# Graph convolution with an LSTM cell on one core: a third dense group, and another layout and order for the span one-hots

## The chip, the cores and the metric

One core of one Trainium2 chip runs the kernel. The metric is the device time of one execution in microseconds (us). The kernel before takes 1732.85 us, the median of 3 runs (1732.84 to 1735.09).

## The reference, cut to what matters

N = 6250 nodes with 256 features, 200,000 edges sorted by destination. The destinations are drawn as `6250 * u ** 2`, so low nodes have most edges: of 25 groups of 250 nodes, group 0 has about 40,000, group 1 16,600, group 2 12,700, group 3 10,700 and group 24 4,000.

```python
agg = segment_sum(x[src], dst, num_segments=N)
h = relu(agg @ W_rel + b_rel + x @ W_root)            # 512 wide
i, f, g, o = split(h @ W_ih.T + b_ih + b_hh, 4)
c = sigmoid(i) * tanh(g)
y = (sigmoid(o) * tanh(c)) @ W_fc + b_fc              # 256 wide
out = layernorm(x + y)
```

## The kernel before, in words

Edges lie in chunks of 128, one edge a partition. A **step** is 4 chunks (QC = 4). A **turn** handles one group of 250 nodes (two tiles of 125); 25 turns run one after the other, and in turn n each engine also does the second half (gates, last layer, layer norm) of the group of turn n - 1.

The sum over a node's edges is made in two ways.

**Tile groups** (23 of 25). GpSimd (POOL) gathers for each step four blocks of 128 rows of x, each split into a high and a low part (four indirect DMAs, L352), into a ring of RING = 7 steps. VectorE (DVE) builds a one-hot of each step against the 125 nodes of the tile (`visit`, L825), and TensorE (PE) multiplies the one-hots with the rows (L424, four matmuls of 512 columns a visit). A tile is done in two parts, so a turn has four parts, in **gaps** j = 0 to 3; a step on a tile's border is visited twice. SyncE forwards the landings (L309). POOL issues step s once PE has begun step s - 7.

**Dense groups** (DENSE = 2: groups 0 and 1). For these PE builds a count matrix `adj` (sources by 250 nodes). A **span** is 5 nodes, a **window** two spans (10 nodes, 25 windows a group), a **pair** one step of a span: DVE makes `rel` (L812), `hot_lo` (128 x 4 chunks, L814) and `hot_key` (245 x 4 chunks, L817), all 16 bit, into a ring of PAIRS = 4. PE multiplies them, four matmuls of 245 columns a pair (L399), into a PSUM bank; a window starts with a clearing matmul (L386) and ends with a marker (L379), and ScalarE (ACT) copies the bank to `adj` (L588). In both tiles the four chunks are innermost, so one chunk's columns lie 8 bytes apart. When the group's 25 windows are done, `product_batch` (L412) multiplies `adj` with x, loaded in 7 batches (896 KB each, `load_batch`) into the space of `hot_key`: batches 0 to 3 in one turn, 4 to 6 in the next, and then comes the dense group's own turn. Each batch is 28 recorded matmuls.

**Order in a gap j of turn n.** PE: `part_sum(j)`, `gates(n-1, j)` (L485, 24 recorded matmuls), the windows of this gap, a batch if there is one. After gap 3: hidden layer (L467, L472), last layer (L493), transposes (L455). DVE: `part_hots(j)`, in gap 0 `normalise(n-2)` (L877 to L888), then `add_high`, `cell_product(n-1, j-1)`, `out_gate(n-1, j-2)` (L846 to L855), and last the windows of the gap (`windows_at`); after gap 3 `norm_stats(n-1)` (L859 to L873), whose sum L864 marks the end of a turn. ACT has the matching order; `store(n-2)` comes after its gap 1. `part_hots` waits until PE has used every one-hot of the part before. Three windows (31 pairs) are built before turn 0.

`SLOTS = (2, 1, 1, 1)` says how many windows each gap of a window turn takes. Counted from the indices, turn by turn (T = tile steps newly consumed, P = pairs in the four gaps, B = batches; 282 steps, 327 visits and 163 pairs in all, POOL issuing 287 steps, a multiple of 7):

```
turn  0: T 25 P 11,4,4,4    turn  7: T 6 (dense 0)        turn 14: T 10 B 3
turn  1: T 21 P 8,4,4,4     turn  8: T 6  P 4,2,2,2       turn 15: T 5 (dense 1)
turn  2: T 19 P 8,4,4,4     turn  9: T 12 P 4,2,2,2       turn 16: T 4
turn  3: T 17 P 6,3,3,3     turn 10: T 12 P 4,2,2,2       turn 17: T 10
turn  4: T 15 P 0,0,2,2     turn 11: T 12 P 4,2,2,2       turns 18-20: T 9 each
turn  5: T 14 B 4           turn 12: T 11 P 4,2,2,2       turns 21-24: T 8 each
turn  6: T 14 B 3           turn 13: T 10 B 4
```

A turn with four parts has T + 2 visits, a turn with two parts T + 1. In group 0 a span has 1 to 9 pairs, in group 1 one pair for nearly all spans.

## Time and profile before

| | |
|---|---|
| median of 3 runs | 1732.85 us |
| the profiled execution | 1737.03 us, span 1735.2 us |
| PE busy / POOL busy / DVE busy / ACT busy | 83% / 73% / 41% / 21% |
| mean granted TensorE clock | 0.915 |

The rows further down come from the page of the profile, from its view by stretches (busy time of each engine between two times), and from its instructions in order of time. PE is TensorE's matmuls, PEld its weight loads. In a row of the timeline, "[1.35 <-DVE hot_key L817]" is the idle time of that engine before the row and what ended it; "x8" is how many instructions the row merges.

Borders of stretches were put at starts of L864, the end of a turn: turn 6 ends at 787.0, turn 8 at 876.7, turn 11 at 1066.8, turn 12 at 1129.7, turn 14 at 1265.3, turn 15 at 1302.1, turn 16 at 1337.9, turn 20 at 1526.3, turn 24 at 1695.9.

### The profile page before, as it was taken

To read this page: it belongs to the slowest core of one execution; us is meant where nothing else is said; L and a number is where in the kernel's file an instruction comes from. 1 tells how busy PE (TensorE), PEld (TensorE's weight loads), DVE (VectorE), ACT (ScalarE), POOL (GpSimd) and SP (SyncE) were. 2 spreads that over 40 slices of the span, in tenths; PEclk is the share of its full clock that TensorE was granted. 3 is DMA by queue.
4 is the path that set the end of the run, shared out by engine and by line. 5 is a ranking of instruction groups with operands and counts; after the bars stand their busy time and mean duration, and the time that the engine had idled before them with its cause. 6 is when DMAs were issued, how large, how long until landed. Compare 5 with 4: busy or idle time off the path is not lost.

```text
span 1735.2 us, 28751 instructions
## 1 busy us (share of the span) xinstructions
PE 1435.9 (83%) x6194; PEld 1128.6 (65%) x6195; DVE 708.4 (41%) x1482; ACT 372.3 (21%) x697; POOL 1263.1 (73%) x1464
## 2 busy tenths in 40 slices
PE   0266557687787789899989889989999999999997
PEld 0133345364555568788777667678888877788886
DVE  8966325255262332213554554422233333333332
ACT  0000011021121221213323223222133222223333
POOL 3668778788787877777757787665763778778772
PEclk9996568798887899899989989999999999999999
DMA  8776676776677778887747667666764677777773
GB/s 272 276 240 183 197 203 192 200 207 187 198 207 199 215 208 270 244 254 218 201 145 216 201 198 216 175 212 213 246 193 120 201 220 213 217 216 214 214 219 90
DMA packets 135705, 360.45 MB, mean 208 GB/s; under 512 B 20207, under 2 KB 58636, under 8 KB 134006
## 3 DMA queue, kind: packets, MB, share of 16 engines
q0 software_dynamic: 91840, 301.01, 59.4%
q10 hardware_dynamic: 39864, 41.96, 7.7%
q1 hardware_dynamic: 3936, 16.62, 2.5%
q8 instruction: 40, 0.66, 0.1%
q14 instruction: 25, 0.20, 0.0%
HBM read 340.31 MB, written 19.20 MB: 207 GB/s over the span
## 4 chain that ended last, share of the span: by engine, by line
PE 34%; POOL 22%; DMA 19%; issue 13%; DVE 6%; DVEq 4%; ACT 1%; POOLq 1%; SPq 0%; ACTq 0%
POOL rows L352 21%; DMA rows<-x_parts,idx 17%; PE ps_blk L485 11%; PE ps_agg L424 6%; PE ps_win L412 4%; PE ps_y L493 3%; PE ps_blk L467 3%; PE ps_blk L472 3%; PE ps_win L399 2%; DMA hot_key<-in_xb 2%; DVEq L812 1%; POOL idx L338 1%; DVE hot_key L817 1%; DVEq L802 1%; DVE rows L694 1%
## 5 line engine op out<-in xcount | busy, mean ns | idle before, releaser
L352 POOL DMA_INDIRECT rows<-x_parts,idx x1148 | 1154.3, 1005 | 398.1 <-issue 320.9
L485 PE MATMUL ps_blk<-cell,wih_sb 128*128 128x250 f32 x2400 | 544.8, 384 | 2.2 <-issue 1.6
L424 PE MATMUL ps_agg<-rows,onehot 128*125 x1308 | 396.8, 454 | 144.6 <-SPq L309 127.0
L485 PEld LDWEIGHTS ps_blk<-cell,wih_sb 128*128 128x128 f32 x2400 | 461.8, 195 | 71.4 <-issue 12.8
L424 PEld LDWEIGHTS ps_agg<-rows,onehot 128*125 128x125 f32 x1308 | 265.3, 209 | 238.4 <-issue 183.9
L825 DVE SCALAR_TENSOR_TENSOR onehot<-iota_f,tile_first,dst_u 128x500 f32 x327 | 242.1, 742 | 328.2 <-PE ps_agg L424 224.5
L613 ACT ACTIVATE cell<-ps_blk,bg_sb 128x250 f32<-128x250 f32 x300 | 140.5, 469 | 526.6 <-PE ps_blk L485 526.6
L399 PE MATMUL ps_win<-hot_key,hot_lo 128*128 x516 | 127.9, 397 | 67.4 <-DVE hot_key L817 60.7
L399 PEld LDWEIGHTS ps_win<-hot_key,hot_lo 128*128 x516 | 59.0, 115 | 126.1 <-issue 90.6
L812 DVE TENSOR_SCALAR rel<-key,span_key x163 | 42.2, 259 | 163.7 <-issue 128.4
L817 DVE TENSOR_TENSOR hot_key<-iota_h,rel 128x980 f16 x163 | 108.0, 663 | 0.1
L467 PE MATMUL ps_blk<-x_t,wroot_sb 128*128 128x250 f32 x400 | 99.1, 380 | 0.1
L472 PE MATMUL ps_blk<-cell,wrel_sb 128*128 128x250 f32 x400 | 94.8, 379 | 0.0
L412 PE MATMUL ps_win<-adj,hot_key 128*128 128x250 f32 x392 | 88.5, 384 | 6.9 <-DMA hot_key<-in_xb 6.9
L493 PE MATMUL ps_y<-wfc_sb,cell 128*125 128x256 f32 x400 | 90.4, 379 | 0.0
L846 DVE TENSOR_TENSOR agg_n<-ps_agg,agg_n 125x256 f32<-125x256 f32 x46 | 19.3, 420 | 170.9 <-ACT agg_n L593 170.9
L412 PEld LDWEIGHTS ps_win<-adj,hot_key 128*128 128x128 f32 x392 | 76.0, 195 | 17.9 <-DMA hot_key<-in_xb 8.8
L850 DVE TENSOR_TENSOR cell<-cell 128x250 f32<-128x250 f32 x100 | 41.9, 419 | 107.6 <-ACT cell L613 107.6
L593 ACT ACTIVATE agg_n<-ps_agg 125x256 f32<-125x256 f32 x46 | 17.6, 383 | 312.8 <-PE ps_agg L379 312.8
L472 PEld LDWEIGHTS ps_blk<-cell,wrel_sb 128*128 128x128 f32 x400 | 73.9, 189 | 12.8 <-ACT cell L597 5.0
L493 PEld LDWEIGHTS ps_y<-wfc_sb,cell 128*125 128x125 f32 x400 | 75.0, 187 | 11.1
L467 PEld LDWEIGHTS ps_blk<-x_t,wroot_sb 128*128 128x128 f32 x400 | 74.3, 192 | 8.9 <-issue 1.0
(113 smaller groups left out, 744.5 us busy)
## 6 DMA issues: line engine op xcount, KB each, us to landing
rows<-x_parts,idx POOLq DMA_INDIRECT x1148, 3.7
hot_key<-in_xb ACTq DMA_DIRECT2D x14, 896.0 KB, 7.2
x_t<-in_xT ACTq DMA_DIRECT2D x25, 250.0 KB, 3.7
x_n<-in_x ACTq DMA_DIRECT2D x25, 250.0 KB
out<-y ACTq DMA_DIRECT2D x25, 250.0 KB
x_parts<-rows SPq DMA_DIRECT2D x6, 1024.0 KB, 4.7
rows<-in_x ACTq DMA_DIRECT2D x8, 512.0 KB, 10.6
x_parts<-wih_sb SPq DMA_DIRECT2D x2, 1024.0 KB, 3.8
```

The lines of the kernel that those rows point to most:

```text
L352: g.indirect_dma_start(rows_f[:, k * QC + j, :], None, x_parts, bass.IndirectOffsetOnAxis(ap=idx[:, k, j:j + 1], axis=0)).then_inc(landed[ ...
L399: last = mm(o, hot_lo[:, ds(half, 1), :, j].squeeze(1), hot_key[:, ds(half, 1), :, j].squeeze(1), start=False, stop=False)
L412: last = mm(ps_win[:, c * GN:(c + 1) * GN], xs[:, b, c * P:(c + 1) * P], adj[:, i * X_BATCH + b, :], start=(i == 0 and b == 0 and c == 0), ...
L424: ins = mm(o, onehot[:, hot * QC + j, 0:TN], rows[:, ds(slot + j, 1), :].squeeze(1), start=(first and j == 0), stop=False)
L467: mm(ps_blk[m % BANKS][:, 0:GN], wroot_sb[:, k, m * P:(m + 1) * P], x_t[:, k, :], start=(k == 0), stop=False)
L472: last = mm(ps_blk[m % BANKS][:, 0:GN], wrel_sb[:, k, m * P:(m + 1) * P], agg_t[:, k, :], start=False, stop=(k == KI - 1))
L485: last = mm(o, wih_sb[:, k, col:col + P], h_t[:, k, :], start=(k == 0), stop=(k == KH - 1))
L493: last = mm(ps_y[0:TN, a * D_OUT:(a + 1) * D_OUT], sig_o[:, k, a * TN:(a + 1) * TN], wfc_sb[:, k, :], start=(k == 0 and a == 0), stop=(k = ...
L613: nc.scalar.activation(dst[:, j, :], ps_blk[b % BANKS][:, 0:GN], fn, bias=bg_sb[:, bias + j:bias + j + 1]).then_inc(gate_done, 1)
L812: v.tensor_scalar(rel[:, ds(half, 1), :].squeeze(1), key[:, ds(c, QC)], span_key[:, at:at + 1] if static else span_key[:, ds(at, 1)], None ...
L817: v.tensor_tensor(hot_key[:, ds(half, 1), :, :].squeeze(1), iota_h[:, :, :], rel[:, ds(half, 1), :].to_broadcast([P, SCOLS, QC]), ALU.is_e ...
L825: v.scalar_tensor_tensor(onehot[:, ds(hot, QC), 0:TN], iota_f[:, 0:TN].unsqueeze(1).to_broadcast([P, QC, TN]), nodes, dst_u[:, ds(c, QC)]. ...
```

## The change

1. DENSE = 3: group 2 is computed by count matrix and product too, its tile steps are gone. There are 25 more windows with 50 pairs, and 7 more batches. TILES falls from 46 to 44 and SPANS rises from 100 to 150, which the table built at the start follows.
2. Group 0's windows go two to each gap (`FIRST_SLOTS`), all others one to each gap.
3. `hot_lo`, `hot_key` and `iota_h` hold two chunks innermost and have an outer dimension of two (PQ) for the other two: a chunk's columns lie 4 bytes apart. The element count of each DVE instruction is as before.
4. DVE builds the windows of a gap directly behind `part_hots`, ahead of `normalise`, `add_high`, `cell_product` and `out_gate`. `normalise` moves to gap 1 and ACT's `store` behind its gap 2.

PE's order within a turn is unchanged. Counted again (258 steps, 301 visits, 213 pairs; POOL issues 259 steps):

```
turn 0: T 22 P 11,8,8,8    turn  7-9: T 12 P 2,2,2,2      turn 16: T 10 P 2,2,2,2
turn 1: T 19 P 8,8,8,7     turn 10: T 11 P 2,2,2,2        turn 17-19: T 9 P 2,2,2,2
turn 2: T 17 P 3,3,6,4     turn 11: T 11 P 2,2,2,4        turn 20: T 8 P 2,2,2,4
turn 3: T 15 B 4           turn 12: T 10 B 4              turn 21: T 8 B 4
turn 4: T 14 B 3           turn 13: T 10 B 3              turn 22: T 8 B 3
turn 5: T 7 (dense 0)      turn 14: T 5 (dense 1)         turn 23: T 4 (dense 2)
turn 6: T 7 P 2,2,2,2      turn 15: T 4 P 2,2,2,2         turn 24: T 4, two parts
```

```diff
-DENSE = 2
+DENSE = 3
-SLOTS = (2, 1, 1, 1)
+FIRST_SLOTS, SLOTS = (2, 2, 2, 2), (1, 1, 1, 1)
+PQ = QC // 2
-            wins = list(SLOTS)
+            wins = list(SLOTS if k > 0 else FIRST_SLOTS)
-        iota_h = sb("iota_h", [P, SCOLS, QC], f16)
+        iota_h = sb("iota_h", [P, SCOLS, 2], f16)
-        hot_lo = sb("hot_lo", [P, PAIRS, P, QC], f16)
-        hot_key = sb("hot_key", [P, PAIRS, SCOLS, QC], f16)
+        hot_lo = sb("hot_lo", [P, PAIRS, PQ, P, 2], f16)
+        hot_key = sb("hot_key", [P, PAIRS, PQ, SCOLS, 2], f16)
...
-                                last = mm(o, hot_lo[:, ds(half, 1), :, j].squeeze(1), hot_key[:, ds(half, 1), :, j].squeeze(1), start=False, stop=False)
+                                last = mm(o, hot_lo[:, ds(half, 1), j // 2, :, j % 2].squeeze(1), hot_key[:, ds(half, 1), j // 2, :, j % 2].squeeze(1), start=False, stop=False)
...
-                    if j == 1 and g2 is not None:
+                    if j == 2 and g2 is not None:
                         store(n - 2, g2)
...
-                    v.tensor_tensor(hot_lo[:, ds(half, 1), :, :].squeeze(1), iota_h[:, 0:P, :],
-                                    src_lo[:, ds(c, QC)].unsqueeze(1).to_broadcast([P, P, QC]), ALU.is_equal)
+                    v.tensor_tensor(hot_lo[:, ds(half, 1), :, :, :].squeeze(1), iota_h[:, 0:P, :].unsqueeze(1).to_broadcast([P, PQ, P, 2]),
+                                    src_lo[:, ds(c, QC)].rearrange("p (q c) -> p q c", c=2).unsqueeze(2).to_broadcast([P, PQ, P, 2]), ALU.is_equal)
                     dve.wait_ge(rel_made, s + 1)
-                    v.tensor_tensor(hot_key[:, ds(half, 1), :, :].squeeze(1), iota_h[:, :, :],
-                                    rel[:, ds(half, 1), :].to_broadcast([P, SCOLS, QC]), ALU.is_equal).then_inc(pairs_ready, 1)
+                    v.tensor_tensor(hot_key[:, ds(half, 1), :, :, :].squeeze(1), iota_h[:, :, :].unsqueeze(1).to_broadcast([P, PQ, SCOLS, 2]),
+                                    rel[:, ds(half, 1), :].squeeze(1).rearrange("p (q c) -> p q c", c=2).unsqueeze(2).to_broadcast([P, PQ, SCOLS, 2]),
+                                    ALU.is_equal).then_inc(pairs_ready, 1)
...
                     if parts[j] is not None:
                         part_hots(t, *parts[j])
-                    if j == 0 and back >= 2:
+                    windows_at(w, wins, j)
+                    if j == 1 and back >= 2:
                         normalise(n - 2)
...
                     if j == KH - 1 and parts[j] is not None and parts[j][1] == 1:
                         add_high(t, parts[j][0])
-                    windows_at(w, wins, j)
```

## Rows read from the trace of the kernel before

**Rows 1.** The page, busy us of each engine with share and instruction count.

```profile
PE 1435.9 (83%) x6194; PEld 1128.6 (65%) x6195; DVE 708.4 (41%) x1482; ACT 372.3 (21%) x697; POOL 1263.1 (73%) x1464
```

**Rows 2.** The page, costliest groups: busy us, mean ns of one | idle before.

```profile
L352 POOL DMA_INDIRECT rows<-x_parts,idx x1148 | 1154.3, 1005 | 398.1 <-issue 320.9
...
L825 DVE SCALAR_TENSOR_TENSOR onehot<-iota_f,tile_first,dst_u 128x500 f32 x327 | 242.1, 742 | 328.2 <-PE ps_agg L424 224.5
...
L399 PE MATMUL ps_win<-hot_key,hot_lo 128*128 x516 | 127.9, 397 | 67.4 <-DVE hot_key L817 60.7
...
L817 DVE TENSOR_TENSOR hot_key<-iota_h,rel 128x980 f16 x163 | 108.0, 663 | 0.1
```

**Rows 3.** View by stretches of POOL's L338 alone, one for each step issued.

```profile
80.60:767.10 686.50, 32.45 (x126) 0.83 0.72 213
226.70:767.10 540.40, 24.39 (x101) 0.86 0.73 214
```

**Rows 4.** View by stretches, all engines: borders, length, PE, PEld, DVE, ACT, POOL, clock, DMA.

```profile
876.70:1066.80 190.10, 173.91 (x768) 133.05 (x766) 91.85 (x204) 54.37 (x93) 143.76 (x168) 0.93 0.68 196
1129.70:1265.30 135.60, 130.12 (x594) 111.95 (x593) 33.81 (x73) 25.65 (x52) 87.08 (x106) 0.97 0.72 223
1265.30:1302.10 36.80, 36.80 (x175) 32.07 (x174) 12.10 (x29) 12.92 (x26) 23.50 (x29) 1.00 0.67 192
1526.30:1695.90 169.60, 165.36 (x762) 139.68 (x761) 62.35 (x136) 51.31 (x104) 134.98 (x161) 1.00 0.74 216
```

**Rows 5.** Timeline of PE in turn 15: start us, us, line, operation.

```profile
1270.70 3.08 PE L424 MATMUL ps_agg<-rows,onehot 128*125 x12
1273.62 10.31 PE L485 MATMUL ps_blk<-cell,wih_sb 128*128 128x250 f32 x48
```

**Rows 6.** Timeline of PE in turn 13, the first two product batches.

```profile
1148.59 9.12 PE L412 MATMUL ps_win<-adj,hot_key 128*128 128x250 f32 x28 [5.30 <-DMA hot_key<-in_xb]
...
1165.55 6.07 PE L412 MATMUL ps_win<-adj,hot_key 128*128 128x250 f32 x28
```

**Rows 7.** Timeline of PE in turn 11, windows of gap 0 and of gap 2.

```profile
1021.49 1.04 PE L399 MATMUL ps_tr<-hot_key,hot_lo 128*128 x4 [1.35 <-DVE hot_key L817]
1024.34 1.04 PE L399 MATMUL ps_tr<-hot_key,hot_lo 128*128 x4 [1.81 <-DVE hot_key L817]
...
1026.55 5.39 PE L424 MATMUL ps_agg<-rows,onehot 128*125 x12 [1.17 <-DVE onehot L825]
...
1047.93 1.92 PE L399 MATMUL ps_win<-hot_key,hot_lo 128*128 x8
```

**Rows 8.** Timeline of DVE in turn 11: normalise, two pairs, two one-hots.

```profile
1011.78 0.17 DVE L877 RECIPROCAL r<-std 125x2 f32<-125x2 f32 x1 [1.01 <-ACT std L622]
...
1014.84 0.23 DVE L812 TENSOR_SCALAR rel<-key,span_key  x1 [1.33 <-issue]
...
1017.41 0.23 DVE L812 TENSOR_SCALAR rel<-key,span_key  x1 [1.23 <-issue]
...
1047.02 0.74 DVE L825 SCALAR_TENSOR_TENSOR onehot<-iota_f,tile_first,dst_u 128x500 f32 x1 [0.42 <-issue]
1048.10 0.74 DVE L825 SCALAR_TENSOR_TENSOR onehot<-iota_f,tile_first,dst_u 128x500 f32 x1 [0.35 <-issue]
```

**Rows 9.** Timeline of DVE before turn 0, two pairs of one span.

```profile
101.26 0.23 DVE L812 TENSOR_SCALAR rel<-key,span_key  x1 [0.32 <-issue]
...
102.79 0.23 DVE L812 TENSOR_SCALAR rel<-key,span_key  x1 [0.32 <-issue]
```

**Rows 10.** One line, L386, 900 to 1130 us: min/median/max ns, first and last start.

```profile
L386 PE MATMUL ps_win<-zero_bf x15: 267/267/268, 910.3 to 1121.5; 128*128 128x245 bf16 x15
```

**Rows 11.** Timeline of DVE at the start, first of four instructions over 100 spans.

```profile
18.15 1.82 DVE L713 TENSOR_TENSOR adj<-chunk_stat,adj 98x1600 f32<-98x1600 f32 x1
```

**Rows 12.** Timeline of DVE, the last two ends of turns.

```profile
1695.94 0.69 DVE L864 TENSOR_TENSOR y<-ps_y,x_n 125x512 f32<-125x512 f32 x1 [3.10 <-PE ps_y L493]
...
1726.32 0.69 DVE L864 TENSOR_TENSOR y<-ps_y,x_n 125x512 f32<-125x512 f32 x1 [1.23 <-PE ps_y L493]
```

More of the change, by code:

```diff
@@ L157, in gnn_kernel @@
         rel = sb("rel", [P, PAIRS, QC], f16)
-        hot_lo = sb("hot_lo", [P, PAIRS, P, QC], f16)
-        hot_key = sb("hot_key", [P, PAIRS, SCOLS, QC], f16)
+        hot_lo = sb("hot_lo", [P, PAIRS, PQ, P, 2], f16)
+        hot_key = sb("hot_key", [P, PAIRS, PQ, SCOLS, 2], f16)
         adj = sb("adj", [P, SRC_HI, GN])
-        xs = hot_key[:, :, :, :].rearrange("p s k c -> p (s k c)")[:, 0:2 * X_BATCH * D_IN].bitcast(f32).rearrange("p (b d) -> p b d", b=X_BATCH)
+        xs = hot_key[:, :, :, :, :].rearrange("p s q k c -> p (s q k c)")[:, 0:2 * X_BATCH * D_IN].bitcast(f32).rearrange("p (b d) -> p b d", b=X_BATCH)
         agg_n = sb("agg_n", [TN, 2, D_IN])
@@ L320, in _ @@
             g.iota(iota_f[:, :], pattern=[[1, P]], base=0, channel_multiplier=0, **imprecise).then_inc(const_made, 1)
-            g.iota(iota_h[:, :, :], pattern=[[1, SCOLS], [0, QC]], base=0, channel_multiplier=0, **imprecise).then_inc(const_made, 1)
+            g.iota(iota_h[:, :, :], pattern=[[1, SCOLS], [0, 2]], base=0, channel_multiplier=0, **imprecise).then_inc(const_made, 1)
             g.memset(zero_bf[:, :], 0.0).then_inc(const_made, 1)
```

## The prediction

> **What bounds the kernel now.** I read the page first: PE is busy 83% of the span and POOL 73% [rows 1], so neither is plainly the bound. POOL's own share misleads: it is busy 1005 ns in each of 1148 gathers [rows 2], but there is a fixed issue time between them. The view by stretches, of the one instruction that POOL runs a step, tells more: 101 steps in 540.4 us, 5.35 us a step, from 227 to 767 us [rows 3]. That is the pace of a POOL that is never held up. The 25 turns then fall in two kinds. Where tile steps times 5.35 us is more than PE's own work, the turn takes POOL's time (turns 21 to 24: 32 steps, 171 us by this rule, 169.6 measured [rows 4]). Where it is less, the turn takes PE's time (turn 15: 5 steps would be 27 us, it takes 36.8 with PE busy throughout at full clock [rows 4]). The reader should see that a group made dense takes steps from POOL and gives work to PE and DVE; so what matters is where in the order each is the bound.
>
> **PE's prices at full clock.** Three visits take 2.92 us (12 matmuls from 1270.70 until L485 starts at 1273.62 [rows 5]), 0.98 each. Turn 15 has 6, so its rest is 36.8 - 5.9 = 30.9 us; with transposes, which a dense turn lacks, 31.5. A product batch is 6.0 us of PE, and the first of a group waited 5.3 for its load [rows 6]: a product is 7 x 6.0 + 5.3 = 47.3. Check: turns 13 and 14 give 2 x 31.5 + 24 x 0.98 + 47.3 = 133.8; measured 135.6 [rows 4].
>
> A window of two ready pairs has 8 matmuls in 1.92 us [rows 7], 0.22 each, with clear and marker about 2.2 us. The same 245 columns take 267 ns from start to end where they lie next to each other [rows 10] and 397 where they lie 8 bytes apart [rows 2]: 130 ns more, about what 245 columns need a second time at 2.4 GHz. So the 8 byte pitch streams at half rate. The change makes it 4 bytes, which no 16 bit row shows. The nearest is the tile matmul: 512 columns of 4 byte words in 0.98 / 4 = 0.245 us [rows 5], full rate. I take full rate, 0.11 a matmul, 1.4 us a window; the other end is no gain, 2.2.
>
> The Trainium skill (SBUF — State Buffer, "Door 1: The DMA port swizzle") says of lines of 16 bytes that two hits on each are enough for full bandwidth. By that the old layout, with two, is already at full rate, and the new one brings nothing; the 397 against 267 ns of the trace speak against it. By the rule the sum would be the second rival's.
>
> **DVE's prices.** Within a span a pair comes every 1.53 us [rows 9]; a span of one pair takes 2.56, since the loop is entered anew [rows 8]. So a window of groups 1 and 2 costs DVE 5.1 us, more than PE. A part of three visits costs 1.0 to enter and 1.1 each [rows 8], 4.3. A normalise is about 2.1 [rows 8], each cell or out operation 0.4. The element counts don't change. The new second input of L814 and L817 repeats one 4 byte word where it repeated 8 bytes. The nearest row: L825 repeats one 16 bit element for each of 125 columns and takes 742 ns for 500 elements [rows 2], about one element a cycle. So I take no extra cost; the other end is 0.5 us a pair (below).
>
> **Part by part.** (a) *Start.* Four instructions over 100 spans of 1.82 us [rows 11] get 150: their length is nearly all elements, so 0.9 us more each, some 3.7 in all. DVE works without a break until x is split, so gathers and pairs start 3.7 later. The smaller `iota_h` saves POOL time that nobody waits for.
>
> (b) *Turns 0 to 11, POOL's.* In 686.5 us POOL issued 125 steps besides the first [rows 3], its early stall at the full ring included. After the change 159 steps are consumed through turn 11. 80.6 + 3.7 + 686.5 + 34 x 5.35 = 952.7. From the last step's issue to the end of its turn there are 20 us (767.1 [rows 3] against the end of turn 6 at 787.0). That makes 973. Turns 0 and 1 now have 35 and 31 pairs: DVE needs 16 x 2.56 + 15 x 1.53 = 64 us for those of turn 1, 27 for its visits and some 11 for normalise, cell operations and layer norm, and only four pairs can be made ahead while PE is in its gates, so about 110 us against POOL's 19 x 5.35 = 102. The ring of 7 takes most of this; I add 5 (bounds 0 and 15): **turn 11 ends at 978**, against 1066.8 before. The other turns stay POOL's: turns 7 to 9 need 64 of POOL and 31.5 + 14 x 0.98 + 5.6 = 50.8 of PE, some 56 of DVE.
>
> (c) *Turns 12 to 24, no longer POOL's.* POOL needs 10 steps or less in each. Turns 12 and 13: 133.8. Turn 14: 30.9 + 6 x 0.98 = 36.8. Turn 15 (5 visits, 4 windows): 31.5 + 4.9 + 5.6, and 2 for DVE, 44. Turn 16 with 12 visits and 4 windows would be 48.9 by PE. But DVE's gap 1 is 4.3 + 5.1 + 2.1 + 0.4 = 11.9 and its gap 2 is 10.6, PE's 2.9 + 5.2 + 1.4 = 9.5. `part_hots` of the next gap is queued behind these, so PE finds no one-hot at gaps 2 and 3, by 1.7 and 1.3 us. That is 52. The same reckoning gives 60 for the turns before of 12 steps, which took 190.1 / 3 = 63.4 [rows 4], so I add 1: 53. Turns 17 to 19: 52 each; turn 20, with two windows in its last gap, 54. Turns 21 and 22: 2 x 31.5 + 20 x 0.98 + 47.3 = 129.9. Turns 23 and 24: 30.9 + 4.9 and 31.5 + 4.9 = 72.2. Sum: 133.8 + 36.8 + 44 + 53 + 156 + 54 + 129.9 + 72.2 = **679.7**, with 2 more for waits on steps as turn 12 begins. The same thirteen turns took 1695.9 - 1066.8 = 629.1 before. DVE's new order costs nothing else: `cell_product` and `normalise` come later, but ACT's tanh and the store are needed only at the turn's end. In gap 0 the build of pairs no longer waits behind `normalise`, and the 1.35 + 1.81 + 1.17 us of idle PE of the double window [rows 7] go.
>
> (d) *Tail.* 1695.94 to 1726.32 and then to the end at 1735.2 [rows 12]: 39.3, unchanged.
>
> Sum: 978 + 681.7 + 39.3 = 1699 us of span, 36 less than 1735.2. The profiled execution took 1737.0 with what lies around its span, the median of runs 1732.85. So the forecast in terms of the median is 1732.85 - 36 = 1697; rounded with the DVE waits being the softer side, **1698 us**. In short: about 89 us saved while POOL is the bound, 53 given back once PE and DVE are.
>
> **Rivals.**
> *One: DVE is not late in turns 15 to 20.* Then these take PE's time: 2 + 4 + 12 + 6 less, and the 5 of turns 0 and 1 go too: 29 less, **1669**. For: `part_hots` could overlap better than I think where slots are free. Against: the same reckoning came out too low before.
> *Two: the layout doesn't do what it says, a matmul stays at 0.22 us.* A window is 0.8 longer; of 25 windows in the PE stage DVE's lateness hides most, 5 to 20 us: **1703 to 1718**. For: no row shows 16 bit columns 4 bytes apart.
> *Three, slower: the repeated single word costs DVE 0.5 us a pair.* The 31 early pairs delay PE, and POOL behind the full ring, by 15.5. Turns 0 and 1, already DVE's, pass on some 20 of their 33. Turns 15 to 20 have 50 pairs, 21 to 25 us. Together 56 to 60: **1754 to 1758**. It decides from 0.3 us a pair on, where the gain of 35 is used up. Against: L825's 742 ns. If the two-at-a-time rate of L817 (980 elements in 663 ns [rows 2]) were lost altogether it would be 0.8 a pair and more, some 1785.
>
> The Trainium skill (Vector Engine (DVE) Microarchitecture Reference, "5.2 Measured stream behaviour on trn2") says that a port keeps its full rate only while elements come in runs of two or more neighbouring 4 byte words. The new repeated input is one such word. By its figures (1.05 against 1.73 ns a column) I estimate 0.5 us a pair: rival three. Whether a word read again counts as a hop no run here shows.
>
> **How the numbers follow.** Forecast 0.52 (own range 1685 to 1715), rival one 0.14, rival two 0.11, rival three 0.15, and 0.08 for a chain that I haven't seen at 1720 to 1740. Faster: 0.52 + 0.14 + 0.11 and half of the last, 0.81; within 0.2% (about 3.5 us, what a measurement of this kernel can tell) 0.03; slower 0.16. Range 1668 to 1745: it leaves out most of rival three and the low edge of rival one.
>
> **What would show it.** Right: L399's mean falls from 397 to some 280 ns; L817 stays near 663; L352 x1036; turn 11 ends near 978 and the thirteen turns after it take about 680; in turns 16 to 20 PE waits for L825 at gaps 2 and 3; POOL's pace is above 5.35 us a step after turn 11. Wrong: L814 or L817 longer, POOL with long stalls before turn 2, or waits for hot_key in the single windows.

## The result

The changed kernel takes 1717.6 us (median; 1711.7 to 1732.5), the kernel before beside it 1733.1. The ratio is 0.991, 95% interval 0.990 to 0.993: 15.5 us faster, where the forecast said 35. The profiled execution has a span of 1716.0 us against 1735.2, 19.2 less. The experiments fall in two sets. In the first (e1 to e6, e9, e10) the kernel before takes 1730 and 1733 us. In the second (e7, e12, e14 to e21) it takes 2242 to 2251 us, on three chips, one of which is the chip of e1 to e4. Between the sets only ratios to the kernel before and single rows are compared here, and an experiment's time is set beside the 1717.6 only in the first set. That comparison is across chips too, so each ratio stands with it.

The page of after (busy us, mean ns of one | idle before), to be read beside [rows 1] and [rows 2]; all line numbers are 1 to 2 higher than before:

```profile
PE 1431.2 (83%) x6531; PEld 1150.2 (67%) x6532; DVE 762.2 (44%) x1604; ACT 395.2 (23%) x720; POOL 1154.3 (67%) x1324
...
L353 POOL DMA_INDIRECT rows<-x_parts,idx x1036 | 1047.7, 1011 | 428.5 <-issue 370.7
...
L400 PE MATMUL ps_win<-hot_key,hot_lo 128*128 x656 | 106.8, 301 | 67.5 <-DVE hot_key L818 61.5
...
L818 DVE TENSOR_TENSOR hot_key<-iota_h,rel 128x980 f16 x213 | 141.2, 663 | 0.0
...
L413 PE MATMUL ps_win<-adj,hot_key 128*128 128x250 f32 x588 | 127.9, 375 | 1.9 <-DMA hot_key<-in_xb 1.6
L815 DVE TENSOR_TENSOR hot_lo<-iota_h,src_lo 128x512 f16 x213 | 113.7, 534 | 1.3 <-issue 1.3
```

POOL gave up 112 gathers and 109 us of busy time. The window matmul fell from 397 to 301 ns, `hot_key` stayed at 663, `hot_lo` rose from 483 to 534.

The view by stretches of after, borders at ends of turns (L866), columns as in [rows 4]. The rows are turns 9 to 11, 12 and 13, 14, 15, 17 to 19, and all of 12 to 24:

```profile
806.20:997.50 191.30, 160.98 (x742) 129.46 (x741) 87.78 (x191) 51.61 (x91) 153.15 (x176) 0.95 0.72 205
997.50:1126.10 128.60, 126.92 (x594) 110.20 (x593) 34.18 (x72) 25.65 (x52) 84.75 (x104) 1.00 0.75 231
1126.10:1163.00 36.90, 36.90 (x175) 32.13 (x174) 12.21 (x30) 12.93 (x26) 22.59 (x29) 1.00 0.67 192
1163.00:1213.50 50.50, 44.06 (x208) 36.33 (x207) 22.61 (x52) 15.96 (x28) 16.59 (x20) 0.93 0.36 100
1266.90:1423.80 156.90, 143.51 (x704) 116.95 (x703) 79.20 (x178) 50.62 (x90) 123.10 (x141) 1.00 0.71 202
997.50:1677.00 679.50, 645.57 (x3063) 545.11 (x3062) 256.06 (x578) 190.37 (x359) 399.28 (x471) 0.99 0.62 181
```

So turn 11 ended at 997.5 instead of the 978 forecast, and turns 12 to 24 took 679.5 against 681.7 forecast. By turns, forecast and measured: 12 and 13 133.8 + 2 and 128.6; 14 36.8 and 36.9; 15 44 and 50.6; 16 53 and 53.3; 17 to 19 156 and 156.9; 20 54 and 58.2; 21 and 22 129.9 and 123.2; 23 and 24 72.2 and 71.9. The tail is 39.0.

POOL's own pace in after, L339 alone, one start for each step issued, as in [rows 3]:

```profile
84.20:782.50 698.30, 33.84 (x126) 0.88 0.73 212
84.20:966.90 882.70, 43.29 (x160) 0.89 0.73 211
```

The forecast put the last of these 160 starts at 952.7; it is at 966.8. Three intervals stand out, 8.5, 7.3 and 9.7 us, behind the ends of turns 1, 3 and 6. The last of them, with PE's first tile matmuls of turn 7, then POOL's next gather:

```profile
687.09 4.05 PE L425 MATMUL ps_agg<-rows,onehot 128*125 x16
...
689.38 0.97 POOL L353 DMA_INDIRECT rows<-x_parts,idx  x1 [4.78 <-issue]
```

Counted from the indices, this gather is of step 108 (the first is 0), which may be issued once PE has begun step 101, the first of turn 7. In all three places the waiting gather starts 2.3 us after PE's first tile matmul of the new turn (360.61 and 362.89, 533.00 and 535.27, 687.09 and 689.38). So POOL stood at the full ring while PE was in the hidden and last layers around the end of a turn. The kernel before has no interval above 6.5 us between 227 and 767 us.

PE in after, turn 17 with the start of its window in gap 3; then the last two windows of turn 11, both in gap 3 (columns as in [rows 7]):

```profile
1280.76 0.27 PE L387 MATMUL ps_win<-zero_bf 128*128 128x245 bf16 x1
1280.86 1.05 PE L400 MATMUL ps_win<-hot_key,hot_lo 128*128 x8
1281.75 0.17 PE L380 MATMUL ps_win<-zero_bf 128*128 128x1 bf16 x1
1283.11 3.24 PE L425 MATMUL ps_agg<-rows,onehot 128*125 x12 [1.20 <-DVE onehot L827]
...
1304.81 2.20 PE L425 MATMUL ps_agg<-rows,onehot 128*125 x8 [1.19 <-issue]
...
1312.63 0.27 PE L387 MATMUL ps_win<-zero_bf 128*128 128x245 bf16 x1
...
1313.77 1.95 PE L468 MATMUL ps_blk<-x_t,wroot_sb 128*128 128x250 f32 x8
```

```profile
984.50 0.27 PE L387 MATMUL ps_win<-zero_bf 128*128 128x245 bf16 x1
...
987.05 0.74 PE L400 MATMUL ps_tr<-hot_key,hot_lo 128*128 x4 [1.27 <-issue]
989.28 0.74 PE L400 MATMUL ps_tr<-hot_key,hot_lo 128*128 x4 [1.48 <-issue]
...
990.37 3.53 PE L468 MATMUL ps_blk<-x_t,wroot_sb 128*128 128x250 f32 x8
```

Two things are to be seen. Eight matmuls of a single window now take 1.05 us instead of 1.92 [rows 7]. Yet the next part starts 2.35 us after the clear (1283.11 - 1280.76), and it was 2.34 before (medians: 8 single windows in turns 9 to 12 before, 15 in turns 16 to 20 after): what the matmuls saved stands as idle time behind the marker, 1.20 us. And a second window in the last gap is dear: 5.87 us from its first clear to the hidden layer, where a single window there takes 1.14, and the hidden layer then runs at half clock, 3.53 us for 8 matmuls instead of 1.95 (granted clock 0.55 from 990.3 to 994.0).

### The profile page after: what moved, and what is told of

Its sections match the earlier page's. It is cut to its first block, busy times and chain, and to the rows that moved or that the text cites. A ratio compares the mean times of both kernels' runs of the same rounds, so it can differ in the third digit from the quotient of the medians.

```text
span 1716.0 us, 30403 instructions
## 1 busy us (share of the span) xinstructions
PE 1431.2 (83%) x6531; PEld 1150.2 (67%) x6532; DVE 762.2 (44%) x1604; ACT 395.2 (23%) x720; POOL 1154.3 (67%) x1324
## 4 chain that ended last, share of the span: by engine, by line
PE 43%; POOL 18%; issue 15%; DMA 12%; DVE 6%; DVEq 5%; POOLq 1%; ACT 0%; SPq 0%; ACTq 0%
POOL rows L353 17%; PE ps_blk L486 17%; DMA rows<-x_parts,idx 11%; PE ps_agg L425 8%; PE ps_win L413 5%; PE ps_y L494 4%; PE ps_blk L468 4%; PE ps_blk L473 2%; PE ps_win L400 2%; DVEq L813 1%; POOL idx L339 1%; DMA hot_key<-in_xb 1%; DVE hot_key L818 1%; PE ps_tr L400 1%; DVE rows L695 1%
## 5 line engine op out<-in xcount | busy, mean ns | idle before, releaser
L353 POOL DMA_INDIRECT rows<-x_parts,idx x1036 | 1047.7, 1011 | 428.5 <-issue 370.7
L425 PE MATMUL ps_agg<-rows,onehot 128*125 x1204 | 344.3, 437 | 117.1 <-SPq L310 78.6
L425 PEld LDWEIGHTS ps_agg<-rows,onehot 128*125 128x125 f32 x1204 | 233.7, 200 | 193.0 <-issue 148.3
L827 DVE SCALAR_TENSOR_TENSOR onehot<-iota_f,tile_first,dst_u 128x500 f32 x301 | 223.1, 743 | 249.0 <-PE ps_agg L425 163.3
L400 PE MATMUL ps_win<-hot_key,hot_lo 128*128 x656 | 106.8, 301 | 67.5 <-DVE hot_key L818 61.5
L818 DVE TENSOR_TENSOR hot_key<-iota_h,rel 128x980 f16 x213 | 141.2, 663 | 0.0
L400 PEld LDWEIGHTS ps_win<-hot_key,hot_lo 128*128 x656 | 64.9, 99 | 105.6 <-issue 84.3
L413 PE MATMUL ps_win<-adj,hot_key 128*128 128x250 f32 x588 | 127.9, 375 | 1.9 <-DMA hot_key<-in_xb 1.6
L413 PEld LDWEIGHTS ps_win<-adj,hot_key 128*128 128x128 f32 x588 | 111.2, 190 | 15.8 <-DMA hot_key<-in_xb 3.3
L815 DVE TENSOR_TENSOR hot_lo<-iota_h,src_lo 128x512 f16 x213 | 113.7, 534 | 1.3 <-issue 1.3
L589 ACT ACTIVATE adj<-ps_win 128x490 f32<-128x490 f32 x62 | 63.4, 1022 | 109.4 <-PE ps_win L380 109.4
## 6 DMA issues: line engine op xcount, KB each, us to landing
rows<-in_x ACTq DMA_DIRECT2D x8, 512.0 KB, 10.7
```

Of the source, the lines that this page charges most:

```text
L353: g.indirect_dma_start(rows_f[:, k * QC + j, :], None, x_parts, bass.IndirectOffsetOnAxis(ap=idx[:, k, j:j + 1], axis=0)).then_inc(landed[ ...
L400: last = mm(o, hot_lo[:, ds(half, 1), j // 2, :, j % 2].squeeze(1), hot_key[:, ds(half, 1), j // 2, :, j % 2].squeeze(1), start=False, sto ...
L413: last = mm(ps_win[:, c * GN:(c + 1) * GN], xs[:, b, c * P:(c + 1) * P], adj[:, i * X_BATCH + b, :], start=(i == 0 and b == 0 and c == 0), ...
L425: ins = mm(o, onehot[:, hot * QC + j, 0:TN], rows[:, ds(slot + j, 1), :].squeeze(1), start=(first and j == 0), stop=False)
L815: v.tensor_tensor(hot_lo[:, ds(half, 1), :, :, :].squeeze(1), iota_h[:, 0:P, :].unsqueeze(1).to_broadcast([P, PQ, P, 2]), src_lo[:, ds(c, ...
L818: v.tensor_tensor(hot_key[:, ds(half, 1), :, :, :].squeeze(1), iota_h[:, :, :].unsqueeze(1).to_broadcast([P, PQ, SCOLS, 2]), rel[:, ds(hal ...
```

## The experiments

**The layout alone taken back (e1).**

```diff
-hot_key = sb("hot_key", [P, PAIRS, PQ, SCOLS, 2], f16)
+hot_key = sb("hot_key", [P, PAIRS, SCOLS, QC], f16)
```
and the same for `hot_lo`, `iota_h` and their readers.

> The kernel after the change with only the layout of the span one-hots put back (four chunks innermost, 8 bytes between columns). Theory of the prediction (a window costs PE its matmuls, 1.4 us with the new layout and 2.2 with the old; PE's work sets turns 12 to 24): 5 to 20 us slower than the 1717.6 of after, 1723 to 1738. Rival (what sets the time from a window's first matmul to the next part's first is PE's own instruction issue, 2.35 us in both traces, so that the matmuls' speed is hidden): 1717 plus or minus 4, with the idle time of PE behind a window falling from 1.2 us to 0.3 while the distance stays 2.3 to 2.4.

Measured 1721.3 us, ratio 0.994 (0.991 to 0.996): 3.7 us more, between the two forecasts, and the two intervals overlap. In the profile each of turns 15 to 20 is 0.7 to 0.9 us longer than in after, 4.7 together, so a few us are what the layout is worth. The page of this run shows the matmul back at the old length:

```profile
L400 PE MATMUL ps_win<-hot_key,hot_lo 128*128 x656 | 160.7, 398 | 62.2 <-DVE hot_key L818 57.4
...
L815 DVE TENSOR_TENSOR hot_lo<-iota_h,src_lo 128x512 f16 x213 | 102.4, 481 | 1.5 <-issue 1.5
```

From clear to next part a single window still takes 2.35 us, with 0.31 idle. So the 54 us of PE time that the layout takes away are off the path for the most part, and the layout is what moves `hot_lo` from 481 to 534 ns.

**VectorE's order alone taken back (e2).**

```diff
                     if parts[j] is not None:
                         part_hots(t, *parts[j])
-                    windows_at(w, wins, j)
-                    if j == 1 and back >= 2:
+                    if j == 0 and back >= 2:
                         normalise(n - 2)
...
                         add_high(t, parts[j][0])
+                    windows_at(w, wins, j)
```
and ACT's store back behind gap 1.

> The kernel after the change with only the order put back: DVE builds a gap's windows last, normalise in gap 0, the store behind gap 1. Theory of the prediction (DVE is behind at gaps 2 and 3 in the new order and the old one has the same sum of work): within 5 us of 1717.6. Rival (the order is worth something, since pairs built last arrive after PE's gates): 1722 to 1735, with PE waiting for hot_key in single windows, above all in turns 16 to 20.

Measured 1747.9 us, ratio 1.009 (1.006 to 1.012): 30 us slower than the changed kernel, more than either theory gave, and slower than the kernel before. In the profile 6.9 us of it lie before the end of turn 11, 23.6 in turns 12 to 24. Turns 16 to 20 take 57.8, 56.2, 57.3, 57.7 and 62.6 us instead of 53.3, 52.5, 52.2, 52.2 and 58.2. PE in turn 17 of this run, gap 0 and gap 3, beside the rows of after above:

```profile
1293.18 0.27 PE L387 MATMUL ps_win<-zero_bf 128*128 128x245 bf16 x1
1293.28 0.61 PE L400 MATMUL ps_win<-hot_key,hot_lo 128*128 x4
1294.59 0.74 PE L400 MATMUL ps_win<-hot_key,hot_lo 128*128 x4 [0.69 <-DVE hot_key L818]
...
1296.80 4.59 PE L425 MATMUL ps_agg<-rows,onehot 128*125 x12 [1.21 <-DVE onehot L827]
...
1327.43 0.27 PE L387 MATMUL ps_win<-zero_bf 128*128 128x245 bf16 x1
...
1328.90 0.78 PE L400 MATMUL ps_win<-hot_key,hot_lo 128*128 x4 [0.77 <-DVE hot_key L818]
...
1329.96 1.95 PE L468 MATMUL ps_blk<-x_t,wroot_sb 128*128 128x250 f32 x8
```

And VectorE in the same gap 0:

```profile
1283.25 2.28 DVE L827 SCALAR_TENSOR_TENSOR onehot<-iota_f,tile_first,dst_u 128x500 f32 x3 [1.90 <-issue]
1287.14 0.17 DVE L879 RECIPROCAL r<-std 125x2 f32<-125x2 f32 x1 [1.61 <-ACT std L623]
...
1290.53 0.23 DVE L813 TENSOR_SCALAR rel<-key,span_key  x1 [1.51 <-issue]
...
1293.07 0.23 DVE L813 TENSOR_SCALAR rel<-key,span_key  x1 [1.23 <-issue]
```

In the old order the second pair of gap 0 begins at 1293.07, when PE already stands at its clear (1293.18). PE waits for `hot_key`; the window takes 3.62 us instead of 2.35, and the 12 matmuls behind it run partly at half clock, 4.59 instead of 3.24 (granted clock 0.63 from 1296.8 to 1301.4, and 1.00 beside it in after). In gap 3 the window takes 2.53 instead of 1.14. Together 1.3 + 1.4 + 1.4 = 4.1 us, against 3.7 by which this turn is longer in all. With three groups the order brings more than the whole gain.

**Five windows a turn in all groups (e3), the old slots.**

```diff
-FIRST_SLOTS, SLOTS = (2, 2, 2, 2), (1, 1, 1, 1)
+FIRST_SLOTS, SLOTS = (2, 1, 1, 1), (2, 1, 1, 1)
```

> The kernel after the change with slots (2, 1, 1, 1) for all three groups, as before the change: five window turns a group instead of three and six. Theory of the prediction (a double window costs two windows more than a single, and 2 us of late DVE each turn; total work is otherwise the same): 1720 to 1732. Rival (what matters is how early PE's work lies, while POOL is the bound): group 0 is finished two turns later, its product moves out of POOL's longest turns, 1725 to 1740.

Measured 1749.7 us, ratio 1.011 (1.008 to 1.013), above both forecasts. Turns 16 to 20 take 55.4, 58.3, 57.7, 57.5 and 57.2 us: a fifth window, which makes one gap a double, costs some 5 us a turn, twice what a single one takes. With three groups the new slots are as much part of the gain as the order, 32 us against 30. With two groups, putting back group 1's slots alone changes nothing (e10, next); group 0's were not tried there.

**Two dense groups with all the rest of the change (e4), and with five windows a turn in group 1 (e10).**

```diff
-DENSE = 3
+DENSE = 2
```
and in e10 also
```diff
-FIRST_SLOTS, SLOTS = (2, 2, 2, 2), (1, 1, 1, 1)
+FIRST_SLOTS, SLOTS = (2, 2, 2, 2), (2, 1, 1, 1)
```

> The kernel after the change with only two dense groups: new layout, new order, two windows a gap in group 0 and one in group 1. It tells the third group from the rest. Theory of the prediction (nearly the whole gain is the third group's, POOL's 24 steps): 1727 to 1735, as the kernel before, since POOL is the bound nearly to the end. Rival (the third group gives nothing, layout and order give the 15 us): 1715 to 1722.

> Two dense groups with the new layout and order, two windows a gap for group 0 and (2, 1, 1, 1) for group 1, so that group 1's product comes a turn earlier than in the run with one window a gap (1702.7). Theory that PE's work should lie early, while POOL is the bound: 1695 to 1701. Rival (a double window's late DVE costs 2 us a turn and takes back what the earlier product gives): 1702 to 1710.

Measured 1702.7 us, ratio 0.983 (0.980 to 0.986), and 1701.1, ratio 0.981 (0.979 to 0.984): the same within their intervals, and both beat both kernels. For e4 both theories were too high, by 12 us and more; e10 lies between its two. The third dense group costs 15 us. In e4 turn 11 ends at 1058.0 and turns 12 to 24 take 603.4. So the third group brings 60.5 us until turn 11 (1058.0 - 997.5) and costs 76.1 after it (679.5 - 603.4): 49 in turns 15 to 20, which take 270.1 in e4 and 319.0 in after, 28 in turns 21 to 24 (166.9 and 195.1), 1 gained in turns 12 to 14.

**Narrower window matmuls (e5)**: three of a pair's four matmuls read 64 columns instead of 245, so it leaves out most counts of three chunks.

```diff
-last = mm(o, hot_lo[...], hot_key[:, ds(half, 1), j // 2, :, j % 2] ...)
+cols = SCOLS if j == 0 else 64
+last = mm(o[:, 0:cols], hot_lo[...], hot_key[:, ds(half, 1), j // 2, 0:cols, j % 2] ...)
```

> The kernel after the change with three of the four matmuls of each pair cut from 245 to 64 columns; most counts of the dense groups are left out, the number of instructions is the same. At full clock a pair's matmuls are 0.23 us shorter, a window's 0.45. Theory of the prediction (PE's streaming sets the window): 25 windows in turns 15 to 20 and some before give 8 to 14 us, 1704 to 1710. Rival (PE's instruction issue sets the distance of 2.35 us from a window's first matmul to the next part's): 1714 to 1719, the idle time behind a window growing from 1.2 to 1.6 us or so with the distance kept.

Measured 1720.1 us, ratio 0.993 (0.991 to 0.996): no gain, 1 us above what the rival gave. From clear to next part it is 2.35 us, with 1.24 idle. Columns don't price the window.

**Half the comparisons (e6)**: VectorE compares two of a step's four chunks, PE reads these two twice (and `is_equal` on `[:, 0:2]` for both one-hots); half the edges of the dense groups are left out.

```diff
-mm(o, hot_lo[:, ds(half, 1), j // 2, :, j % 2]..., hot_key[:, ds(half, 1), j // 2, :, j % 2]...
+mm(o, hot_lo[:, ds(half, 1), 0, :, j % 2]..., hot_key[:, ds(half, 1), 0, :, j % 2]...
```

> The kernel after the change with DVE comparing only two of the four chunks of a pair, so that both comparisons have half the elements (two chunks' counts left out); PE has as many matmuls as before. It tells whether DVE's windows slow POOL's gathers. Theory of the prediction (POOL's pace is its own, 5.35 us a step, and it is only held up by the full ring): turn 11 ends within 3 us of the 997.5 of after. Rival (DVE's comparisons stretch the gathers that run beside them): POOL's pace in turns 7 to 11 falls from 5.44 to 5.38 us or less and turn 11 ends 4 to 10 us earlier; the turns from 16 to 20 stay at 52 to 53 by either.

Measured 1689.8 us, ratio 0.975 (0.972 to 0.979): 28 us faster than the changed kernel, and further than the rival went. Turn 11 ends at 981.4, 16.1 earlier; POOL's starts in turns 8 to 11 are 5.34 us apart instead of 5.44. Turns 12 to 24 take 11.1 less: turns 15 to 20 (48.7 to 53.3 each) 15.2 less, turns 12 and 13 4.2 more. A window's distance falls to 1.7 us. But the edit changes two things: VectorE's work, and the instructions with which PE sets its addresses. They stand in the view of L400 on the queue of the weight loads, first in after, then in e6 (min/median/max ns):

```profile
L400 PEldq FUSED_REGOPS  x852: 74/74/124, 75.1 to 1473.9; - x171
```

```profile
L400 PEldq FUSED_REGOPS  x426: 74/98/124, 75.3 to 1448.6; - x142
```

**PE's half of e6 alone (e12, e16, e20)**: VectorE compares all four chunks, PE reads chunks 0, 1, 0, 1 (half the edges left out again); the edit is the one shown for e6.

> The kernel after the change, DVE's work whole, but PE's four matmuls of a pair read the same two chunks twice (the counts of the other two are left out, those of the first two doubled). The same address work then serves two matmuls, so that PE's sequencer has two of its register instructions fewer a pair, with matmuls and waits as before. It parts the two things that the run with half comparisons changed at once. Theory that PE's sequencer sets the window: distance from a window's first matmul to the next part 1.7 us instead of 2.35, turns 16 to 19 near 50 us, but POOL's pace in turns 7 to 11 still 5.40 to 5.45 a step; 1702 to 1709 in all. Rival (the shorter comparisons of DVE gave all of the 28 us): distance 2.35, 1714 to 1719.

> The changed kernel with one edit: PE's four matmuls of a pair read chunks 0, 1, 0, 1 instead of 0 to 3 (the count matrix is therefore wrong for half the edges of the dense groups). VectorE still compares all four chunks, so its work is whole; PE has as many matmuls with as many columns, but half the address registers to set. Theory A (the 28 us of the run with half the comparisons came from PE's instructions for the addresses): the distance from a window's clear to the next part's first tile matmul falls from 2.35 to about 1.7 us, turns 15 to 20 take some 50 to 51 us, and the time is 1689 to 1698. Theory B (they came from VectorE's comparisons, which are whole here): the time stays at 1714 to 1720. Theory C, both: the 13 turns after turn 11 gain 12 to 16 us and turn 11 still ends near 997, at POOL's pace of 5.43 us a step: 1702 to 1706. I take C as likeliest.

> The changed kernel, PE reading chunks 0, 1, 0, 1 of a pair instead of 0 to 3 (the count matrix is wrong for half the edges of the dense groups); VectorE compares all four chunks as before. Its two runs on chips where the kernel before takes 2240 us showed the distance from a window's clear to the next part at 1.72 to 1.86 us where nothing else held it up, against 2.3 with all four: so PE's instructions for the addresses set that distance. Open is POOL's pace in the turns that it bounds. If VectorE's comparisons alone slow POOL: 5.43 us a step in turns 7 to 11 as in the changed kernel, turn 11 ends at 994 to 999, turns 15 to 20 take 48.5 to 51 us: 1701 to 1706 where the kernel before takes 1733. If PE's shorter windows free POOL too: turn 11 ends near 981 and the time is 1689 to 1695. I take the first. Where the kernel before takes 2240 us again, a ratio near 0.955, and nothing more is learnt.

All three are in the second set: ratios 0.957 (0.952 to 0.963), 0.955 (0.950 to 0.960) and 0.965 (0.961 to 0.968). The changed kernel stands at 0.964 (0.958 to 0.970) there (e19), so these ratios don't decide between the theories. Beside e19 on the same chip e16 is 22 us faster (2136.9 and 2158.5), but so is e17 below (2134.3), whose edit explains only 7 us of its 24; differences of that size aren't understood in this set. A window where nothing else holds PE up does. Of e16, in turn 18:

```profile
1731.19 0.27 PE L387 MATMUL ps_win<-zero_bf 128*128 128x245 bf16 x1
1731.30 1.04 PE L400 MATMUL ps_win<-hot_key,hot_lo 128*128 x8
1732.17 0.17 PE L380 MATMUL ps_win<-zero_bf 128*128 128x1 bf16 x1
1732.92 1.20 PE L425 MATMUL ps_agg<-rows,onehot 128*125 x4 [0.58 <-issue]
```

1.73 us from clear to next part, the median of its 24 single windows in turns 9 to 11 and 16 to 20; the undisturbed ones of e7, which reads all four chunks in the same set, take 2.2 to 2.4. VectorE's work is whole here, so the 0.6 us are PE's own address instructions: two for each pair less, four a window. The records of PE's queue show how. Behind a window PE runs some nine register and table instructions for the next part (from L433 on), 1.35 to 1.39 us from the first of them to the part in after, e1, e5, e6 and e16. That first one starts 0.98 us after the clear in after, 0.97 in e1 and 0.98 in e5, and 0.36 in e6 and e16 (medians). The address instructions start 0.16 us apart, and four of them make this difference. So the distance of 2.35 is PE's queue, the window's part and then the next part's, and the matmuls run beside it. VectorE's half shows in POOL's gathers. All single gathers were sorted by what VectorE ran beside them, for however short a time: alone a gather takes 0.957 us in after (347 of them), beside tile one-hots 1.093 (182), beside `hot_lo` and `hot_key` 1.157 (80). In e6 the last is 1.007 (83), in e16 it is 1.099 (98), as in e7, 1.097 (97). The sorting is rough, since a longer gather meets more of VectorE's work. Among gathers that `hot_lo` or `hot_key` covered for 70% of their length the mean is 1.025 in after (124) and 0.950 in e6 (50), the same way but less. So the shorter window comes from PE's address instructions. That VectorE's shorter comparisons make POOL quicker fits these means, and e6 alone tried it, with PE's windows shorter too. How the 28 us divide between the two causes stays open.

**The 25th window in gap 0 (e9).**

```diff
-                wins[3] += 1
+                wins[0] += 1
```

> The kernel after the change with the odd 25th window of groups 1 and 2 in gap 0 instead of gap 3 (turns 11 and 20 have windows 2, 1, 1, 1). Theory of the prediction (20 us from the last step's issue to the end of a turn, wherever the windows lie): no difference, 1715 to 1720. Rival (turn 11 is the last that POOL bounds, so what PE does behind its last step is on the path: two windows in gap 3 make 31 us of the 20, and in gap 0 the second is hidden behind POOL): turn 11 ends 4 to 7 us earlier, at 991 to 993, and the kernel takes 1710 to 1714.

Measured 1713.0 us, 4.6 less, as the rival said; but the ratio, 0.988 (0.985 to 0.991), overlaps that of after, and the gain isn't clear of noise. In the profile turn 11 takes 60.5 us, where it takes 65.2 in after and 64.4 and 66.8 in e1 and e5, which have the same windows. Yet it ends at 998.6, not at 991 to 993, since turns 3 and 7 are 4.4 and 2.6 us longer in this execution. In turn 20, which POOL doesn't bound, the place is worth 1.1 us (57.1 and 58.2).

**The period loop written out (e7, e17).**

```diff
-with pe.Fori(0, DENSE - 1) as period:
+for period in range(DENSE - 1):
```
and the same on VectorE.

> The kernel after the change with the loop over the dense groups 1 and 2 written out on PE and DVE, so that turn 15 is no longer the start of a second pass of a loop. In after, DVE's first one-hot of turn 15 comes 6.1 us late for no wait that the profile shows, and PE stands 4.2 us. Theory (that is the price of the jump back in a long loop body): turn 15 takes 44 to 46 us instead of 50.6 and the kernel 1711 to 1714. Rival (DVE is late there for another reason, such as a semaphore of the product): turn 15 stays at 50 us and the kernel at 1717.

> The changed kernel with the loop over the two periods written out on PE and VectorE (the same instructions in the same order, without the jump back from turn 14 to turn 15). Theory: VectorE's 6.1 us and PE's 4.2 us of idle time at the start of turn 15 are the jump back, so turn 15 takes 45 to 47 us instead of 50.6, and the time falls by 3 to 6 us, to 1712 to 1715. Rival: the wait there is one for data, or the longer program is fetched just as late where it is straight; then turn 15 stays at 50 to 51 and the time at 1716 to 1720.

Both in the second set: 0.957 (0.950 to 0.965) and 0.953 (0.948 to 0.959) against 0.964 (0.958 to 0.970) of e19. The expected 44 to 47 us for turn 15 belong to the first set; here its difference with and without the loop is what can be read. The place itself is clear. VectorE and PE at the start of turn 15, first in e16 (with the loop), then in e17:

```profile
1530.88 2.30 DVE L827 SCALAR_TENSOR_TENSOR onehot<-iota_f,tile_first,dst_u 128x500 f32 x3 [6.18 <-issue]
...
1531.82 5.42 PE L425 MATMUL ps_agg<-rows,onehot 128*125 x12 [4.26 <-DVE onehot L827]
```

```profile
1523.86 2.46 DVE L827 SCALAR_TENSOR_TENSOR onehot<-iota_f,tile_first,dst_u 128x500 f32 x3 [1.34 <-issue]
...
1525.14 3.12 PE L425 MATMUL ps_agg<-rows,onehot 128*125 x12
```

With the loop turn 15 takes 56.4 and 58.3 us (e12, e16), without it 49.6 and 51.6 (e7, e17). After has the same gap in the first set:

```profile
1171.16 2.29 DVE L827 SCALAR_TENSOR_TENSOR onehot<-iota_f,tile_first,dst_u 128x500 f32 x3 [6.13 <-issue]
...
1172.11 5.48 PE L425 MATMUL ps_agg<-rows,onehot 128*125 x12 [4.21 <-DVE onehot L827]
```

The jump back costs VectorE 4.8 us beyond the 1.34 that it needs anyway, and PE's 12 matmuls behind it run at half clock (5.48 against 3.12, granted clock 0.50 from 1172.0 to 1177.5). On VectorE's queue in after the loop's branch (L941) is at 1164.95 and the next instruction at 1167.86, and 1.7 us more pass a few instructions on, in front of one that takes 0.03. Written out, there is no such gap. Why the first instructions behind the jump come late, no run here shows.

**Two groups in the old order (e14, e18, e21), two groups with the 25th window in gap 0 (e15), and the changed kernel again (e19).**

> Two dense groups, new layout, two windows a gap in group 0 and one in group 1, but DVE's old order. It is the fourth corner of order by number of dense groups. Theory of the prediction (the order costs and gives next to nothing): 1698 to 1708, as with the new order (1702.7). Rival (the order gives some 30 us with three groups and nearly as much with two): 1720 to 1735.

> The changed kernel with two dense groups and the old order of VectorE and of the store; new layout, FIRST_SLOTS and SLOTS (two windows a gap in group 0, one in group 1). It is the fourth corner of a square: three groups with the new order 1717.6, three with the old order 1747.9, two with the new order 1702.7. Theory (what the order brings doesn't hang on the number of dense groups): 1702.7 + 30 = 1728 to 1736. Rival (the order mostly serves the third group, whose windows stand where PE and VectorE are the bound): 1708 to 1716.

> Two dense groups, the new layout and slots, the old order of VectorE and of the store. Where the kernel before takes 1733 us: if the new order brings as much with two groups as with three (30 us), 1728 to 1736, a ratio of 0.997 to 1.002; if it mostly serves the third group, 1708 to 1716. I take the first, since the kernel before, with the old layout beside the old order, stands 30 us above the two groups with the new order. Where the kernel before takes 2240 us, a ratio of 1.01 as the first time.

> Two dense groups, new layout and order, with the 25th window of group 1 in gap 0 instead of gap 3. Theory (the place of the 25th window matters where POOL's stretch ends, which here is turn 11 or 12, and POOL is the bound again at the end, so that what PE gains there is mostly waited away): 1699 to 1704. Rival (as with three groups, 5 us): 1695 to 1699.

> The changed kernel once more, beside the three others on their chip. Where the kernel before takes about 1733 us here, 1714 to 1721 and a ratio of 0.989 to 0.993. Where the chip is one on which the gathers are slower and the kernel before takes some 2240 us, POOL is the bound for longer, and 24 steps fewer are worth more: a ratio of 0.95 to 0.965.

All in the second set. Two groups in the old order: 1.016 (1.011 to 1.022), 1.010 (1.005 to 1.015), 1.013 (1.008 to 1.018); in the new order, with the window in gap 0, 0.990 (0.987 to 0.994); three groups in the new order 0.964 (0.958 to 0.970). e14 and e15 ran side by side, 2269.9 and 2219.7 us. So there the order brings some 2% with two groups too, the place of one window included, and the third group some 2.6% (e19 against e15, across chips, and that window again), where in the first set it costs 0.8% (0.991 against 0.983). With two groups the order wasn't tried in the first set. The expectation of e19 speaks of slower gathers; that is not what the rows show. The page of e7:

```profile
L353 POOL DMA_INDIRECT rows<-x_parts,idx x1036 | 1035.3, 999 | 881.2 <-issue 859.9
```

A gather takes 999 ns, 1011 in after; the idle time ahead of them is 881 us instead of 429. And PE in turn 17 of e7, where one part of 12 matmuls is cut up:

```profile
1684.23 0.73 PE L425 MATMUL ps_agg<-rows,onehot 128*125 x2 [0.29 <-issue]
1685.61 0.47 PE L425 MATMUL ps_agg<-rows,onehot 128*125 x1 [0.65 <-issue]
1688.58 1.03 PE L425 MATMUL ps_agg<-rows,onehot 128*125 x2 [2.50 <-issue]
...
1692.03 7.09 PE L486 MATMUL ps_blk<-cell,wih_sb 128*128 128x250 f32 x24 [0.95 <-issue]
```

PE, and POOL likewise, pause in the middle of their streams, here for 0.3 to 2.5 us, waiting for nothing that the profile shows. POOL loses most: its steps start 7.0 us apart in turns 8 to 11 of e7, 5.44 in after, so that there the 28 steps that the third group takes from POOL pay. That this is the reason is argued from the rows, no run tries it. Why the pauses come, no run here shows.

## Why the prediction was right and wrong

**Right in sign and in range, wrong in the size of the gain**: 35 us forecast, 15.5 measured. The 1717.6 us lie inside the whole range of 1668 to 1745 and just outside the forecast's own, 1685 to 1715.

*The bounds of the turns* were read rightly. Turns to 11 take POOL's time, turns 12 to 24 take PE's; turn 14 took 36.9 (36.8 forecast), turns 23 and 24 71.9 (72.2), the tail 39.0 (39.3).

*Step (b) failed, by 19.5 us.* Three terms were mis-sized. (1) POOL's pace: [rows 3] has 101 starts in 540.4 us, which is 100 intervals, 5.40 us a step and not 5.35: 34 x 0.054 = 1.8 us. (2) The full ring, for which 5 us were allowed and only for turns 0 and 1: the intervals of 8.5, 7.3 and 9.7 us behind the ends of turns 1, 3 and 6, in which POOL waits for PE to begin the next turn, are 9.3 us beyond the pace, and some 3 more are spread over the rest. The last of the 160 starts is 14.1 late, 9.1 after the 5 allowed. (3) The 20 us from that start to the end of the turn were taken from turn 6, which has no windows. Turn 11 has two in its last gap and needs 30.7 (997.5 - 966.8), 10.7 more: 5.9 for the two windows (984.50 to 990.37), 1.6 for the hidden layer at half clock, 0.6 for slower gates, and 2.5 ahead of them, since PE waits 3.9 us for the last step's rows. 9.1 + 10.7 = 19.8, and 19.5 were to be found.

*Step (c) came out within 2.2 us, for the wrong reasons.* A window was taken at 1.4 us of PE. Ahead of a tile part it is 2.35; with those ahead of gates or the hidden layer (1.1 to 1.2) and turn 15's (up to 2.3), the single windows of turns 15 to 20 come to 14.9 more. Their matmuls do run at full rate, but e1 and e5 show that their length doesn't set the distance, and e16 that PE's address instructions do. The tile parts of these turns cost more than 0.98 a visit, 11.0 in all with the markers behind them (turn 17: 12.8 us for 11 visits), a price that was taken from a turn without windows or waits. The second window of turn 20, with the hidden layer at half clock behind it, costs 4.8 more, and the jump back of turn 15 was missing, 6.5. Against these, VectorE was not late at gaps 2 and 3, for which the terms of turns 15 to 20 held 24.1: in turns 16 to 19 PE's idle time ahead of gaps 2 and 3 is 1.06 to 1.28 us, no more than its own queue leaves. The products waited 1.6 and 0.1 us for loads where 5.3 was taken for each, their batches came every 5.72 us instead of 6.0, and the 2 us of turn 12 weren't needed: turns 12, 13, 21 and 22 came out 13.9 lower. 681.7 + 14.9 + 11.0 + 4.8 + 6.5 - 24.1 - 13.9 = 680.9, 1.4 off the 679.5 measured. That the sum of (c) was right is luck, in that misses of 37 and 38 us cancel. Rival one (VectorE not late) was right in its mechanism and far off in its time. Rival two was half right: the matmul does go to full rate, but little of it reaches the end; e1's 3.7 us are short of its lower bound of 5. The reading that it rests on was loose: 245 columns at 2.4 GHz are 102 ns, not the 130 of the rows.

*"DVE's new order costs nothing else"* was the step with the largest single error, though it doesn't enter the sum, since it took the order for a thing of no price. It is worth 30 us with three groups (e2): without it VectorE is late with the pairs in gaps 0 and 3. The working had VectorE's sums for gaps 1 and 2 alone. The sum held because it was made for the new order, but what it says of the third group ("89 us saved, 53 given back") is wrong: with the other edits in place the third group saves 60.5 and costs 76.1. The kernel before didn't tell this: its own turns 12 to 24 take 629.1, 26 more than the 603.4 of e4, which has the new order and slots and the windows of turn 12 already behind it.

*Rival three* was wrong: `hot_key` stayed at 663 ns. The Trainium skill (Vector Engine (DVE) Microarchitecture Reference, "5.2 Measured stream behaviour on trn2") would have a word without a neighbour slow the stream; the trace of after doesn't show that for a word that is repeated. `hot_lo` pays 51 ns (483 to 534), a tenth of what the rival took for the pair. The Trainium skill's rule on lines of 16 bytes (SBUF — State Buffer, "Door 1: The DMA port swizzle") would make the old pitch a full rate one; e1's 398 against 301 ns in after speaks against it.

## What to carry to other kernels

Before more work is moved from one engine to another, ask with one run what the other edits bring without it: here, in the first set, the third dense group cost 15 us, and the reordering beside it brought 30. Price a short group of matmuls by the distance from its first instruction to the next group's, not by the length of its matmuls, and take the distance from a place with the same neighbours. Ask at the end of each turn whether the engine that runs ahead can reach the end of its ring. A stretch with n starts has n - 1 intervals.

## What was not expected of the hardware

- PE runs four address instructions for each pair (74 ns each on the queue of the weight loads, 0.16 us from one start to the next). With two, the window falls from 2.35 to 1.7 us, while matmuls of 64 instead of 245 columns change nothing (e5, e16).
- Two short waits on PE, 0.69 and 1.21 us with a pair's four matmuls between them, are followed by 12 matmuls in 4.59 us at a granted clock of 0.63; in after the wait of 1.20 alone is followed by the same 12 in 3.24 us at 1.00 (e2, turn 17). Waits of 1.27 and 1.48 us in turn 11 of after are followed by 8 matmuls in 3.53 us at 0.55, instead of 1.95.
- A gather issued by POOL takes 0.96 us on average alone and 1.09 to 1.16 where VectorE's one-hots run beside it for some of the time; with 16 bit one-hots of half the length it takes 1.01.
- 512 comparisons of `hot_lo` in the new layout take 534 ns instead of 481, 980 of `hot_key` 663 in both.
- A jump back over a long loop body costs VectorE some 4.8 us.
- The same kernel on the same chip took 1730 us in one set of runs and 2251 in a later one, with pauses in the instruction streams and gathers of the same length; by the ratios the worth of the third dense group changes its sign between the two sets.
